# A macaron block (FFN, attention, FFN) on one core: where each half-step FFN's product is computed

## What is computed

```python
def ffn(y):                       # y = layernorm(x)
    dots = softmax(y @ centroids.T / 0.1)          # 64 clusters
    hits = dots > 0.01
    query_sel, cluster_sel = any(hits, 1), any(hits, 0)
    row_sel = cluster_sel[assignments]             # 1024 outputs
    return where(query_sel[:, None] & row_sel, y @ weight.T + bias, 0)

def attn(y):                      # 32 heads of q, 8 of k and v, D = 32
    q, k, v = y @ Wq + bq, y @ Wk + bk, y @ Wv + bv
    scores = q k^T / sqrt(D)      # 32 x 32 over the features, per token
    return softmax(scores) @ v

x = x + 0.5 * ffn(layernorm(x))
x = x + attn(layernorm(x))
x = x + 0.5 * ffn(layernorm(x))
```

## Time and profile before

| | |
|---|---|
| median of three executions | 1426.45 us |
| lowest, highest | 1422.59, 1429.41 us |
| profiled execution: span from the first to the last instruction | 1418.4 us |
| its own time beside the span | not given apart |
| PE (TensorE matmul) busy | 1328.8 us, 94% |
| DVE (VectorE) busy | 1025.2 us, 72% |
| ACT (ScalarE) busy | 492.7 us, 35% |
| POOL (GpSimd) busy | 180.6 us, 13% |
| DMA | 130.69 MB, mean 92 GB/s |
| instructions | 26718 |

### The profile page before, as it was taken

One profiled execution on the slowest core, in us unless ns is written; L12 is line 12 of the kernel. 1 busy time (PEld: TensorE's weight loads), 2 busy tenths in 40 slices (PEclk: granted clock), 3 DMA queues, 4 the chain that ended last, 5 costly groups with the idle time before them and its releaser, 6 DMA issues. The chain is left out here.

```text
span 1418.4 us, 26718 instructions
## 1 busy us (share of the span) xinstructions
PE 1328.8 (94%) x9360; PEld 1150.8 (81%) x9360; DVE 1025.2 (72%) x1534; ACT 492.7 (35%) x638; POOL 180.6 (13%) x496
## 2 busy tenths in 40 slices
PE   4677799999999999999999999998879999999998
PEld 4666688888888888888888888887768888888887
DVE  5898467898888898888888888897746444444443
ACT  4877224334334334334334334333322111111110
POOL 4555000110110110110110110110000000000000
PEclk9999899999999999999999999999989999999999
DMA  6665013333223323323323323322313222222221
GB/s 220 235 219 178 30 39 83 81 78 80 81 74 78 84 77 78 87 73 81 89 67 77 88 72 78 90 56 67 105 52 119 89 90 90 90 90 90 90 94 48
DMA packets 180364, 130.69 MB, mean 92 GB/s; under 512 B 138608, under 2 KB 157296, under 8 KB 180336
## 3 DMA queue, kind: packets, MB, share of 16 engines
q1 hardware_dynamic: 176112, 126.12, 30.4%
q10 hardware_dynamic: 4224, 4.19, 1.0%
HBM read 79.95 MB, written 50.33 MB: 92 GB/s over the span
## 5 line engine op out<-in xcount | busy, mean ns | idle before, releaser
L178 PE MATMUL ps_a<-w_hi,y_hi 128*128 128x512 f32 x752 | 298.4, 397 | 2.4 <-DVE y_lo L912 2.4
L179 PE MATMUL ps_a<-w_lo,y_hi 128*128 128x512 f32 x752 | 294.2, 391 | 0.0
L180 PE MATMUL ps_a<-w_hi,y_lo 128*128 128x512 f32 x752 | 293.8, 391 | 0.0
L230 ACT ACTIVATE work<-work,norm 128x1024 f32 (+1 forms) x96 | 119.3, 1243 | 254.0 <-POOL norm L218 253.1
L186 PE MATMUL ps_t<-ident,work 128*128 128x128 f32 x1152 | 159.1, 283 | 40.0 <-ACT work L230 34.3
L178 PE MATMUL ps_b<-proj_hi,y_hi 128*128 128x256 f32 (+1 forms) x512 | 181.0, 354 | 0.0
L186 PEld LDWEIGHTS ps_t<-ident,work 128*128 128x128 f32 x1152 | 132.0, 144 | 57.3 <-issue 28.3
L180 PE MATMUL ps_b<-proj_hi,y_lo 128*128 128x256 f32 (+1 forms) x512 | 173.2, 338 | 0.0
L179 PE MATMUL ps_b<-proj_lo,y_hi 128*128 128x256 f32 (+1 forms) x512 | 173.1, 338 | 0.0
L178 PEld LDWEIGHTS ps_a<-w_hi,y_hi 128*128 128x128 f32 x752 | 142.0, 189 | 31.5 <-DVE y_lo L912 2.6
L180 PEld LDWEIGHTS ps_a<-w_hi,y_lo 128*128 128x128 f32 x752 | 141.9, 189 | 30.1
(11 more groups left out here) (145 smaller groups left out, 2227.0 us busy)
## 6 DMA issues: line engine op xcount, KB each, us to landing
work<-in_L_attn_x SPq DMA_DIRECT2D x64, 512.0 KB, 3.3
x_scratch<-work SPq DMA_DIRECT2D x32, 512.0 KB, 2.7
work<-x_scratch SPq DMA_DIRECT2D x32, 512.0 KB, 3.9
out<-work SPq DMA_DIRECT2D x32, 512.0 KB, 2.9
qkv_scratch<-work SPq DMA_DIRECT2D x32, 256.0 KB, 3.3
work<-in_L_ffn_weight SPq DMA_DIRECT2D x8, 512.0 KB, 5.2
work<-in_L_attn_Wq SPq DMA_DIRECT2D x8, 512.0 KB, 5.1
q_head<-qkv_scratch SPq DMA_DIRECT2D x32, 128.0 KB
```

What stands on the lines that cost most here:

```text
L178: pe.matmul(acc, hi[:, k, :], w_h[:, k, cols], start=(k == 0), stop=False)
L179: pe.matmul(acc, hi[:, k, :], w_l[:, k, cols], start=False, stop=False)
L180: last = pe.matmul(acc, lo[:, k, :], w_h[:, k, cols], start=False, stop=(k == KB - 1))
L230: return act.activation(y, x, ACT.Identity, bias=minus_mean_rstd, scale=rstd)
```

## The change

Everything is unrolled in Python: no hardware loops and no register offsets are left. Line numbers from here on are those of the kernel after. What is new, stage by stage:

**Scan.** All eight blocks of W are loaded and prepared at the start (`transpose_rows`). Then each tile's y, while it is there, also gets its first-FFN product (`product_first`, two halves). VectorE adds the bias (`read_first`), Pool multiplies by the token's selection (`select_tokens`), and the result goes to DRAM (f1_d). The cluster softmax is done per pair of tiles. The q, k, v weights are prepared as before, one block per pair. The product of the last tile (31) is computed in iterations 1 and 2 of the attention stage.

**Attention stage.** `load_f` brings the stored first product back; Pool multiplies it by the row mask and adds it to x (`mask_first`, `add_first`); the FFN product, `ffn_half`, and the second norm and transposes for it are gone from this stage. In their place one half product of the second FFN of an even tile is done per iteration, from iteration 4 (`product_third`); ScalarE copies it out and stores it (`store_third`, f3_d). Logits of the second FFN are computed for pairs of tiles, in every second iteration. v is loaded in four DMAs into v_pad and transposed in one VectorE instruction. y_tok and q_diag are one buffer.

**Late stage.** Three more tiles' products (1, 30, 3) are made in the last iterations; 14 tiles (31 and the odd ones from 5) are left. The 18 tiles whose product is ready get mask (Pool), bias and sum (VectorE: `finish_ready`) between them.

The diff, cut to its core:

```diff
-            with eng.Fori(4, NT - 2) as i:
-                emit(i, lambda t: True)
+                for i in range(0, NT + 3):
...
+                    if 0 <= i - 3 < NT:
+                        t = i - 3
+                        sp.wait_ge(o_stored, 16 * (t + 1))
+                        wait(sp, x2, t)
+                        sp.dma_start(o_tok[:, :].rearrange("p (g d) -> p g d", g=HKV), ...).then_inc(o_in, 16)
+                        if t < NT - 2:
+                            sp.wait_ge(x2, t + 1)
+                            sp.dma_start(x2_d[t], x_ring[t % RING][:, :]).then_inc(x2_stored, 16)
+                    if i - 3 >= 0 and i + 1 <= NT + 1:
+                        sp.wait_ge(x2_stored, 16 * (i - 2))
+                        sp.wait_ge(y3, i - 2)
+                        if i + 1 < NT:
+                            load(i + 1)
...
+                    if 0 <= i - 1 < NT:
+                        t = i - 1
+                        sp.wait_ge(qk_read, t + 1)
+                        sp.dma_start(qkv_d[t, 0:2 * HKV]..., qkv_tok[:, 0:2 * HD]...).then_inc(qk_stored, 16)
+                        sp.wait_ge(qk_stored, 16 * (t + 1))
+                        wait(sp, q_ready, t)
+                        sp.dma_start(q_head[:, :], ...).then_inc(q_in, 16)
+                        wait(sp, scores, t)
+                        for r in range(R4):
+                            sp.dma_start(k_diag[32 * r:32 * r + 32, r * HD:(r + 1) * HD], ...).then_inc(k_in, 16)
+                        sp.wait_ge(v_read, t + 1)
+                        sp.dma_start(qkv_d[t, 2 * HKV:3 * HKV]..., qkv_tok[:, 2 * HD:3 * HD]...).then_inc(v_stored, 16)
+                    if i + 2 < NT:
+                        load_f(i + 2)
+                    if 0 <= i - 1 < NT:
+                        t = i - 1
+                        sp.wait_ge(v_stored, 16 * (t + 1))
+                        wait(sp, v_ready, t)
+                        for b in range(T4):
+                            sp.dma_start(v_pad[33 * b:33 * b + 29:4, :], ...).then_inc(v_in, 16)
...
+                def mask_first(t):
+                    pool.wait_ge(f_in, 16 * (t + 1))
+                    pool.tensor_tensor(f_tmp[:, :], f_tmp[:, :], mask[:, :], ALU.mult).then_inc(f_masked, 1)
+                def add_first(t):
+                    pool.wait_ge(x_in[t % RING], 16 * (t // RING + 1))
+                    pool.wait_ge(f_masked, t + 1)
+                    pool.tensor_tensor(x_ring[t % RING][:, :], x_ring[t % RING][:, :], f_tmp[:, :],
+                                       ALU.add).then_inc(x1, 1)
```

More of the change, by code:

```diff
@@ L40 @@
 HKV = HEADS // SCALE
-PROJ = 3 * HKV * D
+HD = HKV * D
+PROJ = 3 * HD
 NCL = 64
@@ L135, in macaron_kernel @@
+        y_tok = q_diag
+        late_base.close()
+        with ExitStack() as stage:
+            slots = [stage.enter_context(nc.sbuf_tensor(f"late{n}", [P, EMB], F32)) for n in range(12)]
+        late_x = slots[0:6]
+        kept_f = slots[3:6]
+        stream_x, stream_f = slots[6:9], slots[9:12]
+        bias_mask = k_diag
+        late_y = [probs, probs_t]
+        part = v_diag
         ps_t = ctx.enter_context(nc.psum_tensor("ps_t", [P, KB, P], F32))
@@ new lines, in fold_logits, with layer_norm_stats @@
+        def fold_logits(pe):
+            for n in range(2):
+                last = pe.matmul(logit_ps[:, n * NCL:(n + 1) * NCL], pair_sums[:, n * P:(n + 1) * P], fold[:, :],
+                                 start=True, stop=True)
+            return last
+        def layer_norm_stats(dve, x, n, t, stats, var, norm, sets=1):
+            dve.bn_stats(bn[n][:, 0, :], x[:, 0:HALF])
+            dve.bn_stats(bn[n][:, 1, :], x[:, HALF:EMB]).then_inc(stats, 1)
+            wait(dve, norm, t + 1 - sets)
+            dve.wait_ge(stats, t + 1)
+            dve.bn_aggr(moments[n][:, :], bn[n][:, :, :]).then_inc(var, 1)
@@ new lines, in select_on, with select_rows, select_mask @@
+        def select_on(dve, n):
+            dve.wait_ge(m_count, n + 1)
+            dve.tensor_scalar(cluster_on[:, :], ps_s[0:NCL, 0:P], 1.0, 0.5, ALU.min, ALU.mult).then_inc(m_on, 1)
+        def select_rows(pe, n):
+            pe.wait_ge(m_on, n + 1)
+            for h in range(2):
+                last = pe.matmul(ps_s[:, half(h)], cluster_on[:, :], onehot[:, half(h)], start=True, stop=True)
+            last.then_inc(m_rows, 1)
+        def select_mask(act, n):
+            act.wait_ge(m_rows, n + 1)
+            act.copy(mask[:, :], ps_s[:, :]).then_inc(m_mask, 1)
@@ new lines, in _ @@
+                act.wait_ge(cen_t, 1)
+                act.copy(cen[:, :, 0:NCL], ps_t[:, :, 0:NCL]).then_inc(cen_hi, 1)
+                norm_first(0)
+                high_first(0)
+                for j in range(4):
+                    high_rows(j)
+                norm_first(1)
+                for j in range(4, 8):
+                    high_rows(j)
+                high_first(1)
+                norm_first(2)
+                copy_pair(0)
+                for j in range(8, 12):
+                    high_rows(j)
@@ new lines, in _ @@
+                pair_soft_exp(act, 0)
+                norm_first(3)
+                for j in range(12, 16):
+                    high_rows(j)
+                for p in range(NP - 1):
+                    for t in (2 * p + 2, 2 * p + 3):
+                        high_first(t)
+                        if p == 1 and t == 4:
+                            pair_soft_exp(act, 1)
+                        if t + 2 < NT:
+                            norm_first(t + 2)
+                    if 2 <= p < KB + 3:
+                        move_kv(p - 2)
+                    if 2 <= p < KB + 2:
+                        high_proj(p - 2)
+                    copy_pair(p + 1)
+                    if p > 0:
+                        pair_soft_exp(act, p + 1)
```

1790 lines of the change are left out of this document (925 added, 865 removed).

## The result

The changed kernel takes 1504.68 us (median of 4 runs, 1498.42 to 1507.71); the kernel before, run beside it, 1427.49 us (1422.59 to 1429.41). The ratio is 1.054 (95% interval 1.0507 to 1.0573): 5.4% slower. I had forecast 1403 us and a range of 1315 to 1458. The profiled execution took 1507.71 us for a span of 1505.9 us.

A forecast was written before the change was run, and what follows sets the result against it. TensorE was to bound the scan and late stage, one SP queue the attention stage: 436 + 61 + 699 + 25.4 + 168 + 4.8 gave a 1395 us span, plus 8 for the median of runs, 1403 us; range 1315 to 1458.

The forecast's parts named there:

- TensorE's work: Whole kernel: some 60 us of work saved and 57 us of idle scan filled, near 130 us if TensorE bounded everything.
- Late stage, 168 us: After the attention stage: 14 x 10.92 + 13 x 0.85 + 4 us of TensorE work, with VectorE's 122 us hidden.
- SP loop, 23.3 us an iteration: Attention stage: one SP queue's stores, landings and loads, with VectorE's steps, set 23.3 us against TensorE's 19.45.
- the output loop: Attention stage: the path past probabilities, heads, o store and o_tok load, a lower bound of 20.9 us an iteration.
- the v_pad issues: Attention stage, SP queue: four v_pad loads replace one v_head load, at 0.47 us each, 1.9 us an iteration.
- The landing of v: Attention stage, SP queue: from the v store to its landing, counted as 3.8 us of each iteration.
- The 0.4 that I took off for loop registers: Attention stage, q/k store to v store: an estimated 0.4 us saved by registers no longer computed, leaving 5.85 us.
- the 0.25 for more traffic: Attention stage: 0.25 us added per iteration because 2.7 MB pass instead of 2.1.
- Scan, 436 us: Scan: first product at 23 us, then 403.5 us of work, 5 for low clock and 5 for late folds.
- The fold waits: Scan: fold_pair waits for ScalarE's copy_pair, 0 to 1 us late in 8 pairs, 5 us in all.
- Pool's lock: Attention stage: Pool's mask product holds the port when L967 starts; 2.4 us more per iteration, 25.7, 1475 us; chance 0.20.
- First rival: Attention stage: TensorE or the output loop sets the pace, 19.45 to 20.9 us an iteration, 1288 to 1331 us; chance 0.20.

The follow-up runs named there:

- experiment 9: Its last kernel: all edits together, with late tiles 4 to 6 loaded early into free buffers and the third kept tile back in its place: 1351.84 us, ratio 0.9497.
- experiment 1: Changed kernel with the late stage's x2 load issued ahead of the prepared tiles' stores in SP's order: 1441.64 us, ratio 1.010.
- experiment 3: Changed kernel with the o_tok load moved ahead of the four v_pad loads, still behind the wait for v's landing: 1453.95 us, ratio 1.021.
- experiment 7: Changed kernel with copy_pair ahead of the projection's copies in ScalarE's order in the scan: 1493.98 us, ratio 1.0476.
- experiment 8: Changed kernel with Pool's token multiply given two inputs instead of one input and a per-partition scalar: 1496.79 us in one run.
- experiment 2: Changed kernel with the o_tok load ahead of the wait for v's landing in SP's order: 1462.22 us, ratio 1.0251.
- experiment 5: Kernel with both loads moved (1397.74 us), plus Pool's product with the mask put behind the second norm factors: 1379.25 us, ratio 0.9679.

## Why the prediction was wrong, step by step

- **TensorE's work** was right in amount: a pair of tiles in the scan takes 25.97 us where nothing waits (26 forecast). The busy time fell by 25 us and not by some 60, and the low clock behind the stops goes with the difference: in experiment 9's last kernel, with the same 8776 matmuls at a mean granted clock of 0.99, it is 1259.6 us, 69 less than before.
- **Late stage, 168 us** (TensorE's work alone, with VectorE's "122 of 168 us: hidden"). This step failed, and it is 81 of the 111 us. I compared amounts per engine and stopped there. The loads of this stage, their place in SP's queue and the store ahead of each were not followed, though for the attention stage I had done just that. The real bound was a loop of 18.2 us a tile; experiment 1 removes it and gives 186.6, and with the buffers of experiment 9 it is 177.9.
- **SP loop, 23.3 us an iteration.** Right in place and size (23.56 between adds), but partly by luck. Only the iterations without a pair ran over SP, at 23.6 on average; those with one ran mostly over the output loop, at 22.9, which I had bounded at 20.9. In the one read above (22.85), TensorE starts at the low clock after waiting for the third norm (to the next block 1.62 us for the transposes instead of 0.85, 4.25 for the v product instead of 3.05) and has the pair's logits ahead of the heads; I had left both out. The transposes take 1.97 us in 8 of the 15 iterations with a pair, so the low clock is not in all of them, and no run separates it from the logits. Of my terms the v_pad issues were 2.7 and not 1.9. The landing of v is no serial term, since o lands beside it (experiment 3). The 0.4 that I took off for loop registers and the 0.25 for more traffic are shown by no run: the whole step from the q/k store to the v store took 6.0 in the iteration read, where I had 5.85 with the 0.4 taken off.
- **Scan, 436 us.** The first product began at 28.2 and not 23: 5 us. The fold waits were named, with 0 to 1 us in eight pairs; the eight periods were 1.5 us longer each, so 12 us and not 5. Behind them stands the price of the token multiply: I wrote that it "can only be less" than two-input rows, and it was 2.86 us where the two-input products took 2.14. Experiments 7 and 8 each take these waits away or shorten them. The two are 12 of the 14.8 us.
- **Pool's lock**, the second rival, did not occur at L967 (1.23 us in all 32). The margin held because the o_tok load was so late; experiments 2 and 5 show the lock as real as soon as that load is early.
- **First rival** (the output loop sets the pace, 19.45 to 20.9): what the iterations fall to once SP is out of the way, 20.3 without a pair, 22.6 with one in experiment 5.
- **The range** ended at 1458. It had no case in which the late stage was anything but TensorE's. With a late stage of 168 the span would have been 1425: the other errors together (+30) had already used up the whole gain I forecast.

So the expected gain was there, and it was given back by the order in one queue: two loads in another place turn 5.4% slower into 1.9% faster, and with the other edits into 5.0% faster (ratio 0.9497). That the kernel with both loads moved, 1397.74 us, lies near my 1403 is luck: its iterations are 22.0 us and not 23.3, which pays for a scan and a late stage that are longer than in my sum.

## What to carry to other kernels

When a change adds a stage that is meant to be covered by TensorE, follow its loads as well as its arithmetic: for each load, what stands ahead of it in its queue, and what the store there waits for. If that wait leads back to the tile the last load brought, the stage runs at the length of that loop, whatever the engines' busy shares say. And two waits in one queue add up only if their transfers do not run side by side; ask what else is landing at the time.

## What the runs showed of the hardware that I had not expected

- On Pool, a multiply of 128x1024 fp32 by a per-partition value took 2.86 us as tensor_scalar, 1.89 us as tensor_tensor with that value broadcast, and 2.14 us as tensor_tensor with a full second tile (means over 31, 31 and 32 instructions). The Trainium skill (GPSIMD Engine Reference, section Engine selection) says that operations with one input run roughly at line rate there and those with two at about half of VectorE's speed. The second half fits these rows (2.14 us, where VectorE's add of two such tiles takes 1.23). The first doesn't: the form with one tensor input is the slowest of the three, and the measurement decides.
- Pool's sum in the attention stage (L606) takes 2.94 us on average against 2.14 for its product with the mask. It runs beside a VectorE pass with two SBUF inputs (L995); that this is the reason was not tested. VectorE waited 7.6 us for the sum in the whole kernel.
